# GpSimd modulates the first slice's rows, TensorE meets modulated router weights, and the first slice's scatter is spread over three product groups

## The reference

```python
mod = (silu(c) @ wmod).reshape(16, 6, 1, -1)      # sa, ca, ga, sb, cb, gb for each of 16 batches
h = layernorm(x) * (1 + ca) + sa
x = x + ga * attention(h)                         # gated delta rule, a scan over 256 time steps
h = layernorm(x) * (1 + cb) + sb                  # "the second modulation"
logits = h @ router_w + router_b                  # 8 experts, one of them for each row
x = x + gb * expert(h) * max_prob                 # each row through the expert it is routed to
```

## Time and profile before

| | us |
|---|---|
| median of 3 runs | 469.03 |
| lowest and highest | 467.74, 471.08 |
| the profiled execution | 469.78 |
| its span, first to last instruction | 468.0 |

### The profile page before, as it was taken

One profiled execution on the slowest core, in us unless ns is written; L12 is line 12 of the kernel. 1 busy time (PEld: TensorE's weight loads), 2 busy tenths in 40 slices (PEclk: granted clock), 3 DMA queues, 4 the chain that ended last, 5 costly groups with the idle time before them and its releaser, 6 DMA issues.

```text
span 468.0 us, 8624 instructions
## 1 busy us (share of the span) xinstructions
PE 368.5 (79%) x2495; PEld 317.9 (68%) x2495; DVE 377.9 (81%) x1143; ACT 281.0 (60%) x634; POOL 276.6 (59%) x339
## 2 busy tenths in 40 slices
PE   3867853938779996993867866879989999999970
PEld 2322410728567766993967866879888999999970
DVE  4859999999998999999997999976828445569634
ACT  3589766956357466586646626374774657566520
POOL 1036234999999949757678198704185556653340
PEclk9989987878879999898698796999999999999995
DMA  8184888992000002923200004117411114155006
GB/s 229 39 118 94 109 114 119 137 127 3 0 1 1 1 1 90 373 78 66 71 0 1 1 7 117 60 41 162 150 30 41 41 41 115 46 164 139 28 34 179
DMA packets 49502, 37.13 MB, mean 79 GB/s; under 512 B 11088, under 2 KB 45200, under 8 KB 49328
## 3 DMA queue, kind: packets, MB, share of 16 engines
q1 hardware_dynamic: 46064, 30.39, 32.9%
q0 software_dynamic: 3392, 6.18, 4.3%
HBM read 17.36 MB, written 10.29 MB: 59 GB/s over the span
## 4 chain that ended last, share of the span: by engine, by line
PE 32%; DVE 30%; POOL 13%; issue 11%; ACT 7%; DMA 6%; SPq 1%; ACTq 0%; POOLq 0%; DVEq 0%
PE bank L900 9%; PE bank L636 6%; DVE U L1797 6%; DVE S L1810 5%; DVE p L1791 5%; DVE p L1804 4%; PE bank L917 4%; PE bank L693 3%; POOL sorted_h L1085 3%; POOL big L1019 2%; DMA sorted_h<-X,pos 2%; POOL prod_o L308 2%; ACT ph L1197 2%; PE bank L638 1%; PE bank L697 1%
## 5 line engine op out<-in xcount | busy, mean ns | idle before, releaser
L693 PE MATMUL bank<-prod_o,ID 128*128 128x128 f32 x512 | 75.5, 308 | 30.3 <-POOL prod_o L315 18.4
L900 PE MATMUL bank<-Q,p 128*128 128x128 f32 x736 | 94.2, 275 | 1.2 <-ACT p L1507 1.2
L693 PEld LDWEIGHTS bank<-prod_o,ID 128*128 128x128 f32 x512 | 70.5, 219 | 33.1 <-POOL prod_o L315 21.7
L900 PEld LDWEIGHTS bank<-Q,p 128*128 128x128 f32 x736 | 89.0, 192 | 1.5 <-ACT p L1507 1.4
L1312 ACT ACTIVATE p<-S,GAM 128x64 f32<-128x64 f32 x126 | 48.4, 410 | 66.9 <-DVE S L1810 66.2
L308 POOL TENSOR_TENSOR prod_o<-Q,ST 128x1024 f32<-128x1024 f32 x28 | 60.0, 2143 | 29.4 <-PE bank L697 29.2
L1143 POOL DMA_INDIRECT placed_y<-Q,place x46 | 44.4, 965 | 49.4 <-DVE place L2003 17.9
L1507 ACT ACTIVATE p<-big 128x1024 f32 x46 | 48.5, 1057 | 40.9 <-PE bank L900 38.9
L1810 DVE TENSOR_REDUCE S<-p 128x64 f32<-128x320 f32 x126 | 55.8, 475 | 0.0
L1797 DVE TENSOR_REDUCE U<-p 128x32 f32<-128x288 f32 x128 | 52.2, 442 | 0.0
L1791 DVE TENSOR_TENSOR p<-S,bank 128x256 f32<-128x256 f32 x128 | 48.7, 410 | 0.7 <-ACT bank L1307 0.7
(11 more groups left out here) (265 smaller groups left out, 746.1 us busy)
## 6 DMA issues: line engine op xcount, KB each, us to landing
big<-in_L_ffn_w_dram SPq DMA_DIRECT2D x1, 4096.0 KB, 14.1
big<-big SPq DMA_DIRECT2D x16, 192.0 KB, 4.5
Q<-sorted_h SPq DMA_DIRECT2D x46, 64.5 KB, 2.2
sorted_h<-ZERO SPq DMA_DIRECT2D x2, 1472.0 KB, 17.8
X<-in_L_attn_x_dram SPq DMA_DIRECT2D x8, 256.0 KB, 4.6
big<-big SPq DMA_DIRECT2D x16, 128.0 KB, 5.4
K<-placed_y SPq DMA_DIRECT2D x8, 256.0 KB, 3.2
out_dram<-X SPq DMA_DIRECT2D x8, 256.0 KB, 2.4
```

The lines of the kernel that those rows point to most:

```text
L693: pe.matmul(ps, ID[:, :], prod_o[:, k % 2, i, :], start=(i == 0), stop=False, skip_group_check=True)
L900: m = pe.matmul(bank[(1, 6)[g % 2] + k][:, c * P:(c + 1) * P], W1E[g % 2][:, f:f + P], XST[:, g % 3, :], start=True, stop=True)
```

## The change

For slice one, `modulate_rows` on GpSimd, after product (11,1), takes the place of the modulation of turned columns; `turn_back`, `rows`, `shift2` and `shift_rows` go. ScalarE only copies the turned tiles (`copy_turned_first`), and TensorE weighs them against the modulated router weights, with the product of ones first. `modulate_router` moves from behind the scan to GpSimd's place after product (7,1). Scales and shifts of slice one are spread by SP earlier: both shifts once the scaled outputs exist, both scales once the attention of slice one is summed; the broadcast of a shift among the experts goes. `H2T` is in another tile. Logits are asked one chunk earlier (52 for 53), the sort too (54 for 55). The scatter's bursts come after products (12,1), (13,0) and (13,1).

```diff
-    AT_SHIFT = (AT_ROWS + 2, AT_ROWS + 4)
-    SHIFT_AT = {AT_ROWS + 3: (1,), AT_ROWS + 4: (3,)}
-    H2_AT = {AT_ROWS + 3: (0,), AT_ROWS + 4: (1,), AT_ROWS + 5: (2,), AT_ROWS + 6: (3,)}
-    AT_ROUTE, AT_SORT, AT_EXP = AT_ROWS + 5, AT_ROWS + 7, AT_ROWS + 10
+    TURNED_AT = {AT_ROWS + 3: (0, 1), AT_ROWS + 4: (2, 3)}
+    AT_ROUTE, AT_SORT, AT_EXP = AT_ROWS + 4, AT_ROWS + 6, AT_ROWS + 10
     BURSTS = ((0, 6, 11, NT), tuple(range(0, NT + 1, 4)))
...
-        SHIFTS = [K_[1][:, 0:P, :].rearrange("p t d -> p (t d)").rearrange("p (n d) -> p n d", n=HB),
-                  K_[0][:, P:2 * P, :].rearrange("p t d -> p (t d)").rearrange("p (n d) -> p n d", n=HB)]
-        SCALES = [PD[h][:, :, :].rearrange("p c t -> p (c t)").rearrange("p (n d) -> p n d", n=HB) for h in range(NHALF)]
+        SHIFTS = [K_[h][:, 0:P, :].rearrange("p t d -> p (t d)").rearrange("p (n d) -> p n d", n=HB) for h in range(NHALF)]
+        SCALES = [[flatx[h][:, 0:HB * D].rearrange("p (n d) -> p n d", n=HB) for h in range(NHALF)],
+                  [PD[h][:, :, :].rearrange("p c t -> p (c t)").rearrange("p (n d) -> p n d", n=HB) for h in range(NHALF)]]
...
-        H2T = K_[0][:, 0:P, :].rearrange("p t d -> p (t d)").rearrange("p (r t) -> p r t", r=2)
+        H2T = sm[:, 0:4, :].rearrange("p x t -> p (x t)").rearrange("p (r t) -> p r t", r=2)
...
                 else:
-                    queue.wait_ge(sem("att_ps", 0), 4)
+                    queue.wait_ge(sem("h2_evac"), 4)
...
             sp.wait_ge(sem("mod_rows"), 32)
-            sp.wait_ge(sem("ov_ready1_", 0), 1)
-            spread_rows(0, 0, SHIFTS[0])
+            for h in range(NHALF):
+                sp.wait_ge(sem(f"ov_ready{h}_", 0), 1)
+                spread_rows(h, 0, SHIFTS[h])
+            sp.wait_ge(sem("att_ps", 0), 4)
+            for h in range(NHALF):
+                spread_rows(h, 1, SCALES[0][h])
             for h in range(NHALF):
                 sp.wait_ge(sem("prod_ready", h), PG)
                 sp.wait_ge(sem("weights_in"), NHALF)
-                spread_rows(h, 1, SCALES[h])
+                spread_rows(h, 1, SCALES[1][h])
...
                     move_outputs(sp, 1, [1])
-                    spread_rows(1, 0, SHIFTS[1])
...
                 s, q = divmod(k, 4)
                 if s == 0 and q >= 2:
-                    pe.wait_ge(sem("router_in"), 4 * (q - 1))
+                    pe.wait_ge(sem("router_in"), 2 + 4 * (q - 1))
                 elif s == 0 or q < 2:
                     pe.wait_ge(sem("xn2_ready", s), 4 * (q + 1))
                 if k == 0:
                     pe.wait_ge(sem("x1_ready", 0), 4)
                 if s == 0 and q >= 2:
-                    shifted(pe, k - 2)
+                    pe.wait_ge(sem("turned_in"), q - 1)
...
                 s, q = divmod(k, 4)
                 if s == 0:
-                    shifted(pe, k)
+                    pe.wait_ge(sem("turned_in"), q + 1)
...
-                if k == 4:
-                    pe.wait_ge(sem("router_in"), NT // 2 + 2)
+                if q == 0:
+                    pe.wait_ge(sem("router_in"), 2)
                     pe.matmul(LG_BANK[s], ONES[:, :], RWS[0].rearrange("p b e -> p (b e)"), start=True, stop=False, skip_group_check=True)
                 for i in range(4):
                     t = 4 * q + i
                     lg_t = LG_BANK[s][:, t * E:(t + 1) * E]
-                    if s == 0:
-                        m = pe.matmul(lg_t, H2T[:, k % 2, i * P:(i + 1) * P], RW[:, :], start=True, stop=True)
-                    else:
-                        m = pe.matmul(lg_t, H2T[:, k % 2, i * P:(i + 1) * P], RWS[1][:, t, :], start=False, stop=True, skip_group_check=True)
+                    m = pe.matmul(lg_t, H2T[:, k % 2, i * P:(i + 1) * P], RWS[1][:, t, :], start=False, stop=True, skip_group_check=True)
                 m.then_inc(sem("lg_ps"), 1)
 
-            def turn_back(k):
-
-                s, q = divmod(k, 4)
-                if s == 0 and k >= 1:
-                    pe.wait_ge(sem("h2_evac"), k)
-                for i in range(4):
-                    m = pe.transpose(BACK_BANKS[s][q][:, i * P:(i + 1) * P], H2T[:, k % 2, i * P:(i + 1) * P], ID[:, :])
-                m.then_inc(sem("h2_ps"), 1)
...
             def rank(s):
 
                 pe.wait_ge(sem("oh_ready"), s + 1)
-                if s == 0:
-                    pe.wait_ge(sem("h2_evac"), 4)
-                else:
+                if s == 1:
                     pe.wait_ge(sem("act_rows"), NT // 2 + 3)
...
                 if g == G_TURN:
-                    for q in range(3):
+                    for q in (0, 1):
                         turn_rows2(q)
-                    weigh_experts(0)
-                    turn_back(0)
-                    turn_rows2(3)
-                    weigh_experts(1)
-                    turn_back(1)
+                    for q in (0, 1):
+                        weigh_experts(q)
+                        turn_rows2(2 + q)
                     for q in (2, 3):
                         weigh_experts(q)
-                    for q in (2, 3):
-                        turn_back(q)
...
@@ -1058,10 +1036,13 @@
                 h, first = q // 2, q % 2 * 4
                 rows = H2[s][h][:, first:first + 4, 0:D]
                 pool.wait_ge(sem("xn2_ready", s), NT // 2)
-                pool.wait_ge(sem("act_rows"), NT // 2)
-                if k == 4:
-                    pool.wait_ge(sem("mod_rows"), 32 + 16 * 4)
-                link(pool.tensor_tensor(rows, XNB[:, 4 * q:4 * q + 4, :], SCALES[h][:, first:first + 4, :], ALU.mult))
+                if s == 0:
+                    pool.wait_ge(sem("router_in"), 2 + NT // 2)
+                else:
+                    pool.wait_ge(sem("act_rows"), NT // 2)
+                if q == 0:
+                    pool.wait_ge(sem("mod_rows"), 32 + 16 * (4 + 2 * s))
+                link(pool.tensor_tensor(rows, XNB[:, 4 * q:4 * q + 4, :], SCALES[s][h][:, first:first + 4, :], ALU.mult))
                 pool.tensor_tensor(rows, rows, SHIFTS[h][:, first:first + 4, :], ALU.add).then_inc(sem("h2_evac"), 1)
...
                 for h in range(NHALF):
                     make_products(pool, g, h)
                     if g == G_SORT:
-                        if h == 0:
-                            place_rows(0)
-                        sort_rows(0, h)
-                if g == G_SORT:
-                    sort_rows(0, 2)
+                        sort_rows(0, 1 + h)
+                if g == G_SORT - 1:
+                    sort_rows(0, 0)
+                if g == G_TURN + 1:
+                    place_rows(0)
+                    for q in range(4):
+                        modulate_rows(q)
...
+                if g == G_SCALE - 1:
+                    modulate_router()
                 if g == G_SCALE:
...
-            modulate_router()
             move_outputs(pool, 1, [0], range(SHARE, HB), "ot_pool")
...
                 if g >= PG:
-                    act.wait_ge(sem("shifted"), 16)
                     dst = bank_states(g, h)
...
-            def rows(k):
-
-                s, q = divmod(k, 4)
-                act.wait_ge(sem("h2_ps"), k + 1)
-                act.activation(H2[s][q // 2][:, q % 2 * 4:q % 2 * 4 + 4, 0:D], BACK_BANKS[s][q][:, :].rearrange("p (n d) -> p n d", n=4), ACT.Copy)\
-                    .then_inc(sem("h2_evac"), 1)
...
-            def shift_rows(k):
-
-                act.wait_ge(sem("xn2t_ps"), k + 1)
-                act.wait_ge(sem("shifted"), 4 * k)
-                if k >= 2:
-                    act.wait_ge(sem("h2_ps"), k - 1)
-                for i in range(4):
-                    b = 4 * k + i
-                    act.activation(H2T[:, k % 2, i * P:(i + 1) * P], TURN_BANKS[0][k][:, i * P:(i + 1) * P], ACT.Identity,
-                                   scale=MOD[:, 3, b:b + 1], bias=MOD[:, 2, b:b + 1]).then_inc(sem("shifted"), 1)
+            def copy_turned_first(q):
+
+                act.wait_ge(sem("xn2t_ps"), q + 1)
+                if q >= 2:
+                    act.wait_ge(sem("lg_ps"), q - 1)
+                act.activation(H2T[:, q % 2, :], TURN_BANKS[0][q][:, :], ACT.Copy).then_inc(sem("turned_in"), 1)
...
-                for q in SHIFT_AT.get(n, ()):
-                    shift_rows(q)
-                for q in H2_AT.get(n, ()):
-                    rows(q)
+                for q in TURNED_AT.get(n, ()):
+                    copy_turned_first(q)
...
-            def shift2(k):
-
-                dve.wait_ge(sem("xn2t_ps"), k + 1)
-                if k >= 2:
-                    dve.wait_ge(sem("shifted"), 4 * k)
-                    dve.wait_ge(sem("h2_ps"), k - 1)
-                for i in range(4):
-                    b = 4 * (k % 4) + i
-                    dve.tensor_scalar(H2T[:, k % 2, i * P:(i + 1) * P], TURN_BANKS[k // 4][k % 4][:, i * P:(i + 1) * P],
-                                      MOD[:, 3, b:b + 1], MOD[:, 2, b:b + 1], ALU.mult, ALU.add).then_inc(sem("shifted"), 1)
...
```

(9 more changed lines are left out.)

## The result

The changed kernel takes 471.08 us (median of 15 runs, 469.52 to 472.58) where the kernel before, run beside it, takes 469.70 (median of 15, 467.65 to 471.08). The ratio is 1.0036, its 95% interval 1.0020 to 1.0052: about 1.7 us slower, 0.9 to 2.4, so well inside 1%. The forecast was 472.0, range 467.0 to 474.5.

The account below looks back on a forecast made before the run. No engine full; VectorE's scan bounds 236 to 303 us. VectorE gains 2.5 before the port, but GpSimd's (13,1) ends 4.4 later and its sums delay (14,1) and (15,1): 469.78 + 2.2 = 472.0 us, range 467.0 to 474.5.

Parts of the forecast that it names:

- two excursions: Chain of waits, 236 to 303 us: leaves VectorE's scan for TensorE's sums of (10,1) at 245.44 and last sums from 301.47.
- the 0.55 for the ranks: VectorE's wait at 268.45: claimed to go, since TensorE no longer turns anything back before the ranks.
- The new way to the logits: Turned tiles go TensorE, ScalarE copy, TensorE router weights, with two slots; VectorE waits 3.4 for logits, until 256.3.
- The port: Four VectorE routing instructions with two SBUF inputs each wait half a GpSimd modulation instruction: 2.5 lost, bounds 0 and 5.1.
- What had been costed at nothing: Ahead of (13,1): router's product before (8,0), covered by GpSimd's 7.89 wait, 0.8 if uncovered; broadcasts landed by 256.8.
- The sums of (13,1): TensorE's sums of product group 13, half 1: kept at their slow 4.36, ending at 298.5; bounds 2.70 and 5.25.
- VectorE's (14,1): VectorE's product group 14, half 1, awaiting the sums of (13,1): starts at 298.6 instead of 296.47, 2.1 late.
- The sum of + 2.2: Total step taken from + 2.1 at (14,1) and + 2.3 at (15,1); everything behind keeps its length.
- The other figure, 471.2: Forecast time when started from the median of the runs, 469.03, instead of the profiled 469.78.
- the port was not held in full: Rival: port holds VectorE a whole GpSimd instruction each time, 5.1 lost, end 1.5 later still, 473.5; chance 0.13.
- Rival 1: VectorE keeps a gain if the sums of (13,1) end before 296.4: 1.3 us, 468.5; whole 2.5, 467.3; chance 0.18.
- The burst 5.5 sooner: GpSimd's first scatter burst starts at 273.4 against 278.89; five more scatters ahead of (13,1) end that product 4.4 later.

Follow-up runs that it names:

- run 4: Changed kernel with slice one's best logit, comparison and first hit in PSUM, so no routing instruction reads two SBUF tiles; one time, 470.75 us.
- run 6's second kernel: Changed kernel with 22 unused matmuls on TensorE ahead of the sums of (13,1); ratio to the kernel before 1.0019 (0.9994 to 1.0044).
- run 1: Changed kernel with the second burst of five scatters moved behind GpSimd's product (13,1); ratio to the kernel before 0.9972 (0.9950 to 0.9993).
- run 2: Changed kernel with its scatter bursts where the kernel before has them; ratio to the kernel before 0.9958 (0.9939 to 0.9977).
- runs 5, 7 and 8: Changed kernel with logits a chunk later: alone 1.0028; with second burst behind (13,1) 0.9975; with bursts as before 0.9954; ratios to the kernel before.
- run 6's first kernel: Changed kernel with 14 unused matmuls on TensorE ahead of the sums of (13,1); ratio to the kernel before 1.0018 (0.9994 to 1.0042).
- Run 8: Changed kernel with bursts where the kernel before has them and logits in chunk 53 again; ratio to the kernel before 0.9954 (0.9932 to 0.9975).

## Why the prediction was right, point by point

- **The chain before**: read as almost wholly VectorE's from 236 to 303 us, with two excursions. It has a third, of 11 us, over ScalarE and TensorE:
```profile
257.75 0.16 ACT K L1400
...
259.31 1.17 PE bank L792 x8
...
268.45 0.42 DVE RT L1874
```
VectorE worked all that while and waited for it only at its end, the 0.55 for the ranks, which the prediction has as a term. So the sum did not suffer.

- **The new way to the logits**: 3.4 of waiting worked out, 3.08 measured. The wait for the ranks went, as said.
- **The port**: 2.5 taken with bounds of 0 and 5.1; the four rows show 1.25 in all (0.80 + 0.28 + 0.87 + 0.43 less four of 0.28). Two were held for about half of a GpSimd instruction (0.52 and 0.59), as taken; one started between two of them and one met only a tail (0.15). That the end does not depend on it was right (run 4).
- **GpSimd**: iotas to first modulation 253.97 - 253.42 = 0.55, taken as 0.8; modulation 264.08 - 253.97 = 10.1, taken as 10.0; first scatter at 270.91 + 2.48 = 273.4, as said; six scatters 278.38 - 270.91 = 7.5, as said; five scatters 287.91 - 281.83 = 6.1 where 6.25 stood. The product of (13,1) ends at 291.2 + 2.48 = 293.7, said 294.1: 4.0 later than before, said 4.4. What had been costed at nothing ahead of it cost nothing: GpSimd's first modulation did not wait for the broadcasts, and the 7.89 of idle time behind the router's product still were 7.35.
- **The sums of (13,1)**: the term that was sized too small. 294.83 + 1.20 - 291.25 = 4.78 instead of 4.36. TensorE stood 5.10 before them, where about 4 had been said and 2.09 had been before; that the longer standing made the difference is not shown (the last section has sums that do not go by it). That the product ended 0.4 sooner and the sums took 0.4 longer, so that the two cancel, is luck.
- **VectorE's (14,1)**: said 298.6, measured 296.07 + 2.48 = 298.55; **(15,1)**: said 306.5, measured 303.90 + 2.48 = 306.4. The sum of + 2.2 came out as 2.21, against the one profile of before; by time it is 1.7 (0.9 to 2.4).
- **The time**: 472.0 went out from 469.78, and this start was good: run beside the changed kernel, the kernel before has 469.70. The step was somewhat large, 2.2 for 1.7. The other figure, 471.2, is nearer to the 471.08 by luck: its start, 469.03 of three runs, was 0.7 low.
- **The rivals**: VectorE did not keep its gain, and the port was not held in full. Rival 1's condition, the sums of (13,1) done before 296.4, was not met (298.5). How near it was, run 6's second kernel shows: with sums of 2.9 the loss in the profile is 0.35.
- What the argument left out: that the two parts of the change can be priced apart. "The burst 5.5 sooner" was one result of GpSimd's order; run 1 and run 2 show that rows as rows with the scatter behind (13,1) are a gain of 1.3 to 2.0.

## What to carry to other kernels

An indirect scatter is work for the engine that issues it: here 1.26 us of GpSimd each. Put ahead of a product that another engine must sum before a third may reuse its slot, five of them cost some 3 us (after against run 1, 1.0036 and 0.9972), and behind it they cost nothing that shows until their own result becomes the last to come. When a wait is taken from an engine, look for the next place at which it meets the engine that sets the pace: here, in runs 5, 7 and 8, some 3 us of VectorE only moved from one wait to another (2.5 to 2.8). A change of two parts is worth trying part by part, for a gain can be hidden under a loss.

## What the runs showed of the hardware that was not expected

A group of 24 sum matmuls took 4.78 in after, 2.9 in run 6's second kernel and, after standing 1.71, 4.0 in run 1. The windows view of after has at this place (the stretch in us, its length; busy time and instructions of PE, PEld, DVE, ACT and POOL; the granted clock of TensorE as a share of full speed; the share and GB/s of DMA):
```profile
291.00:295.00 4.00, 3.75 (x17) 3.75 (x18) 1.35 (x4) 0.00 (x0) 3.12 (x4) 0.50 0.51 163
...
299.00:304.00 5.00, 5.00 (x48) 5.00 (x47) 3.89 (x11) 1.93 (x4) 0.00 (x0) 1.00 0.45 97
```
and in the run with 22 unused matmuls ahead of the sums:
```profile
291.00:295.00 4.00, 3.90 (x35) 3.77 (x34) 2.16 (x5) 0.86 (x3) 3.10 (x4) 1.00 0.55 168
```
The granted clock was 0.50 (1.2 GHz) up to 295 us, for most of the sums, after TensorE had stood 5.10, and 1.00 (2.4 GHz) where it had worked up to them. In run 1 standing 1.71 was followed by 0.73 on average from 296 to 300, and in run 6's first kernel the sums were slow again after 1.98. A late producer can thus be paid twice in the profile: by its lateness, and by the slower sums behind it, here 1.9 us. It is paid only where another engine waits for the sums: in run 2 those of (13,1) took 5.3 after standing 3.85, and VectorE did not wait.

Standing right before does not decide alone, as TensorE's timeline in run 1 shows:
```profile
245.08 2.02 PE L689 MATMUL bank<-prod_o,ID 128*128 128x128 f32 x16 [2.84 <-ACT K L1326]
...
254.97 3.76 PE L689 MATMUL bank<-prod_o,ID 128*128 128x128 f32 x16
```
Here the sums of (10,1), after 2.84 of standing, took 2.8, at a granted clock of 1.00; in after, with the same 2.84, they took 4.3. In run 1 the clock fell to 0.50 only from 254 to 260, with TensorE at work, and there the sums of (11,0), right behind other matmuls, took 5.3. Run 8 shows the same. So the pairing of late products and slow sums is that of most groups in these profiles, not of every execution; whether it is part of the spread of the times was not tried.
